# Straight-line batches and a re-ordered batch head in a two-layer graph kernel

## What is computed

```python
feats = einsum('bnf,hfu->bhnu', X, W)              # 8 heads of 64
dense = leaky_relu(e_self[..., :, None] + e_neigh[..., None, :], 0.2)
att = softmax(dense + -1e10 * (1 - A))             # e_* = feats . a_*
out = relu(einsum('bhij,bhju->bhiu', att, feats) + b)
x = layernorm(x + out)
agg = einsum('bij,bjf->bif', adj, x) / max(sum(adj), eps)
x = layernorm(x + relu(einsum('bnf,of->bno', concatenate([x, agg]), W)))
```

## Time and profile before

| | |
|---|---|
| median of 3 runs | 3521.29 us (3521.27 to 3525.59) |
| the profiled execution | 3527.3 us, its span 3525.3 us |
| PE busy | 3383.6 us, 96% of the span |
| DVE / ACT / POOL busy | 2466.5 / 1870.4 / 284.8 us |
| mean granted TensorE clock | 0.985 of full speed |

### The profile page before, as it was taken

The page is one execution under the profiler, slowest core; times in us unless marked ns, Lnnn a source line. Parts: engine busy times, 40 slices in busy tenths (PEclk is TensorE's granted clock), DMA queues, the critical chain, the costliest instruction groups (busy, mean ns, idle before and its releaser), DMA issues.

```text
span 3525.3 us, 135227 instructions
## 1 busy us (share of the span) xinstructions
PE 3383.6 (96%) x58432; PEld 2881.7 (82%) x58432; DVE 2466.5 (70%) x4364; ACT 1870.4 (53%) x2457; POOL 284.8 (8%) x252
## 2 busy tenths in 40 slices
PE   5999999999999999999999999999999999999998
PEld 4978879787796878969789697887978879788795
DVE  4857668576685766858578585784857758577685
ACT  3736546365464645646456373563746547355463
POOL 0020200202001020010201002010020200202001
PEclk9999999999999999999999999999999999999999
DMA  4113131131321213112031221312213121131210
GB/s 170 52 43 117 39 103 56 50 99 38 103 64 55 93 35 106 64 54 93 29 113 57 67 81 32 117 50 81 68 37 119 43 97 52 44 116 39 85 34 25
DMA packets 98401, 248.46 MB, mean 70 GB/s; under 512 B 14720, under 2 KB 14720, under 8 KB 97792
## 3 DMA queue, kind: packets, MB, share of 16 engines
q1 hardware_dynamic: 97792, 239.38, 20.5%
HBM read 205.26 MB, written 34.08 MB: 68 GB/s over the span
## 4 chain that ended last, share of the span: by engine, by line
PE 85%; DVE 8%; issue 5%; ACT 1%; DMA 0%; SPq 0%; DVEq 0%; ACTq 0%; POOL 0%; POOLq 0%
PE six L887 70%; PE pair L887 10%; DVE xs L766 2%; DVE stats L771 2%; PE six L1023 2%; DVE feat L658 1%; PE pair L916 1%; PE six L916 1%; PE pair L924 1%; PE six L924 1%; DVE rs L779 0%; ACT x_parts L502 0%; DVE trl L647 0%; DVE nb L781 0%; DVE x_parts L636 0%
## 5 line engine op out<-in xcount | busy, mean ns | idle before, releaser
L887 PE MATMUL six<-rest,mask 128*128 128x65 bf16 x16384 | 1549.8, 195 | 4.2 <-issue 4.0
L887 PE MATMUL six<-x_parts,mask 128*128 128x65 bf16 x16384 | 1549.4, 192 | 1.9 <-issue 1.3
L887 PE MATMUL six<-third,mask 128*128 128x65 bf16 x16384 | 1549.3, 192 | 0.2
L887 PEld LDWEIGHTS six<-x_parts,mask 128*128 128x128 fp8e4 x16384 | 1536.0, 97 | 8.9 <-issue 7.6
L887 PEld LDWEIGHTS six<-third,mask 128*128 128x128 fp8e4 x16384 | 1536.6, 98 | 0.0
L887 PEld LDWEIGHTS six<-rest,mask 128*128 128x128 fp8e4 x16384 | 1530.7, 96 | 6.9 <-issue 5.6
L479 ACT ACTIVATE step<-s_bc,n_step 128x1024 uint16<-128x1024 f32 x1024 | 1093.5, 1137 | 382.1 <-DVE mask L716 381.8
L716 DVE TENSOR_TENSOR mask<-adj_t,step 128x1024 uint16<-128x1024 uint16 x1024 | 651.3, 685 | 22.6 <-ACT step L479 22.6
L887 PE MATMUL six<-adj_t,x_parts 128*128 128x512 fp8e4 x1536 | 388.1, 380 | 7.1 <-ACT x_parts L502 5.6
L422 POOL TENSOR_TENSOR s_bc<-feat,rden 128x512 f32<-128x512 f32 x112 | 123.9, 1111 | 2998.0 <-DVE s_bc L759 2969.2
L887 PEld LDWEIGHTS six<-adj_t,x_parts 128*128 128x128 f16 x1536 | 146.4, 98 | 184.8 <-issue 23.6
(11 more groups left out here) (124 smaller groups left out, 4954.1 us busy)
## 6 DMA issues: line engine op xcount, KB each, us to landing
s_bc<-self_scores SPq DMA_DIRECT2D x128, 512.0 KB, 3.7
adj_nat<-in_adj_dram SPq DMA_DIRECT2D x96, 512.0 KB, 3.8
xs<-in_x_dram SPq DMA_DIRECT2D x128, 256.0 KB, 2.8
out_dram<-mask SPq DMA_DIRECT2D x128, 256.0 KB, 3.3
adj_nat<-in_x_dram SPq DMA_DIRECT2D x64, 256.0 KB, 5.0
step<-in_x_dram SPq DMA_DIRECT2D x64, 256.0 KB, 3.6
mask<-in_adj_dram SPq DMA_DIRECT2D x32, 512.0 KB, 5.0
xs<-in_L_gnn_W_dram SPq DMA_DIRECT2D x1, 2048.0 KB, 11.2
```

What stands on the lines that cost most here:

```text
L887: return pe.matmul(o, l, r, start=start, stop=stop, skip_group_check=True)
```

## The change

1. No engine loops over batches: each engine's code for the 16 batches is written out one after the other. With the loops the register arithmetic of the waits goes, and the `stand` increments are removed from all engines.
2. PE's batch begins with `features(b, 4)` (it waits for `o_sum` of tile 6 of the batch before, which frees bank 4), then `scores(b, 1)` in bank 5 in place of 6, then `features(b, 5)` in bank 6 in place of 5, in pieces: two chunks, the 8 transposes, one chunk, the small product (bank 3 in place of 6), the last chunk. The waits for `o_sum` and `o2_sb` of the last tile stand ahead of `features(b, 5)`, not at the end of the batch before.
3. `turn_x1(0)` comes after tile 2 of `aggregate_first`, not after tile 1.
4. DVE does `x_low(b + 1, 7)` before the sum of `ln1(7)`, not behind it.

```diff
-    FT_BANKS = (0, 1, 4, 5, 4, 5, 4, 5)
+    FT_BANKS = (0, 1, 4, 5, 4, 6, 4, 5)
+    SC_BANKS = (6, 5)
+    MAX_BANK = 3
...
-                dve.tensor_copy(nmax[:], bank[6][:, 0:SC]).then_inc(chain.sem, tick())
+                dve.tensor_copy(nmax[:], bank[MAX_BANK][:, 0:SC]).then_inc(chain.sem, tick())
...
+                    if more and t == T - 1:
+                        x_low(b + 1, T - 1)
                     dve.wait_ge(o2_sb.sem, o2_sb.at(b, t + 1))
                     dve.tensor_tensor(z[:, s], bank[O1_BANKS[s]][:], o2s[:, s], ALU.add).then_inc(o_sum.sem, 1)
-                    if more and t == T - 1:
-                        x_low(b + 1, T - 1)
...
             def batch(b, more):
 
+                if b >= 1:
+                    pe.wait_ge(o_sum.sem, o_sum.at(b - 1, T - 1))
+                features(b, 4)
+                pe.wait_ge(ft_sb.sem, ft_sb.at(b, HALF))
+                scores(b, 1)
+                if b >= 1:
+                    pe.wait_ge(o_sum.sem, o_sum.at(b - 1, T))
+                    pe.wait_ge(o2_sb.sem, o2_sb.at(b - 1, T))
                 pe.wait_ge(sc_f32.sem, sc_f32.at(b, 1))
-                scores(b, 1)
-                features(b, 4)
+                features(b, 5, range(0, 2))
                 pe.wait_ge(sc_f32.sem, sc_f32.at(b, 2))
-                stand(pe)
                 for t in range(T):
                     ins = pe.transpose(bank[2][:, t * SC:(t + 1) * SC], sc_row[:, col(t)], ident[0:SC, 0:SC])
                 ins.then_inc(nat_ps.sem, 1)
+                features(b, 5, range(2, 3))
                 pe.wait_ge(diag_ok.sem, diag_ok.at(b, 1))
-                mm(bank[6][:, 0:SC], ones16[:], diag16[:], True, True).then_inc(max_ps.sem, 1)
-                features(b, 5)
+                pe.wait_ge(at_sb.sem, at_sb.at(b, T - 1))
+                mm(bank[MAX_BANK][:, 0:SC], ones16[:], diag16[:], True, True).then_inc(max_ps.sem, 1)
+                features(b, 5, range(3, KC))
...
-                    if jt == 1:
+                    if jt == 2:
...
-                    pe.wait_ge(o2_sb.sem, o2_sb.at(b, T))
-                    pe.wait_ge(o_sum.sem, o_sum.at(b, T))
...
-            with pe.Fori(0, B - 1) as b:
-                batch(b, True)
-            batch(B - 1, False)
+            for b in range(B):
+                batch(b, b + 1 < B)
```

More of the change, by code:

```diff
@@ L358, in _ @@
                 load_late_adj(0, t)
-            with sp.Fori(0, B - 1) as b:
+            for b in range(B - 1):
                 first_scores(b)
@@ L466, in score_rows @@
                 half = slice(i * HALF * P, (i + 1) * HALF * P)
-                copy(sc_row[:, half], bank[6][0:SC, :]).then_inc(sc_f32.sem, 1)
+                copy(sc_row[:, half], bank[SC_BANKS[i]][0:SC, :]).then_inc(sc_f32.sem, 1)
             def batch(b, more):
@@ L574, in _ @@
                 degrees(0, t)
-            with act.Fori(0, B - 1) as b:
-                batch(b, True)
-            batch(B - 1, False)
+            for b in range(B):
+                batch(b, b + 1 < B)
         @block.vector
@@ L879, in _ @@
                 adj_rows(0, t)
-            with dve.Fori(0, B - 1) as b:
-                batch(b, True)
-            batch(B - 1, False)
+            for b in range(B):
+                batch(b, b + 1 < B)
         @block.tensor
@@ L926, in turn_adj, with features @@
                 ins.then_inc(at_ps.sem, 1)
[L928 to L931, removed]
-                c = t % HALF
-                split_product(bank[FT_BANKS[t]][:], [trh[:, k, col(c)] for k in range(KC)],
-                              [trl[:, k, col(c)] for k in range(KC)], [w0h[:, k, :] for k in range(KC)],
-                              [w0l[:, k, :] for k in range(KC)]).then_inc(ft_ps.sem, 1)
+            def features(b, t, chunks=range(KC)):
+                if 0 in chunks:
+                    pe.wait_ge(xt_lo.sem, xt_lo.at(b, t + 1))
+                    if t >= 4:
+                        pe.wait_ge(ft_sb.sem, ft_sb.at(b, t - 1))
+                c = t % HALF
+                ins = split_product(bank[FT_BANKS[t]][:], [trh[:, k, col(c)] for k in chunks],
+                                    [trl[:, k, col(c)] for k in chunks], [w0h[:, k, :] for k in chunks],
+                                    [w0l[:, k, :] for k in chunks], first=0 in chunks, last=KC - 1 in chunks)
+                if KC - 1 in chunks:
+                    ins.then_inc(ft_ps.sem, 1)
             def scores(b, i):
                 pe.wait_ge(xt_lo.sem, xt_lo.at(b, (i + 1) * HALF))
-                split_product(bank[6][:], [wah_wide[:, k * SC:k * SC + P] for k in range(KC)],
+                split_product(bank[SC_BANKS[i]][:], [wah_wide[:, k * SC:k * SC + P] for k in range(KC)],
                               [wal_wide[:, k * SC:k * SC + P] for k in range(KC)],
```

14 lines of the change are left out of this document (removed).

## The result

The kernel after takes **3409.6 us** (median of 4 runs, 3404.98 to 3412.62) against 3521.61 us before (4 runs, 3521.27 to 3525.59): the ratio is 0.9678, with an interval of 0.9662 to 0.9695. Forecast were 3406 us, in a range of 3392 to 3430. The profiled execution took 3408.76 us, of which 3406.6 us are its span; before, the span was 3525.3 us. So there are 118.7 us of span to account for.

What follows compares the result with a forecast made beforehand. PE, busy 96% of the span, was taken as the bound, with stops and slow clock at batch borders. Gains 102.2 + 3.4 + 12.5 - 3 = 115.1 us off 3527.3 give 3412, less 6.0 for the median: 3406 us, range 3392 to 3430.

Steps and rivals of the forecast that it cites:

- The term of the heads: Batch starts on PE: 102.2 us gained at 14 looped borders, 3.4 at the last, 0 at batch 0.
- The new head: PE from last adjacency transposes to first key product: no stop left, full clock, 15.2 us (bounds 14.9 to 15.74).
- the sign: Evidence that would show the forecast right: total PE busy lower by some 25 to 30 us as slow products go.
- The split of a border: Looped batch borders on PE: 3.85 us of each come from the jump, 3.45 from the order.
- The loops of the other engines at nothing: DVE, ACT and SP in their loops: slack exceeds the cost, so straight code there gains nothing.
- DVE, ACT and SP have slack: Key tiles: PE takes 1.5 us a tile, these engines have more slack than register work costs; gain nothing.
- The register arithmetic: Register work and `stand` in the key tiles: removal gains nothing, as batch 15 without registers keeps the same pace.
- `turn_x1(0)` one tile later: Second layer on PE: tile 2's aggregations cover a wait; 0.89 us in 14 batches, 12.5 us gained (bounds 0 to 13.4).
- The masks uncovered: First key tiles, tightest at tile 7: less cover for masks from scores through DRAM; 0.2 us a batch, 3 us lost.
- The rival that the masks become the bound: First key tiles: scores' DRAM trip makes all late by 1.3 us, not 0.2; 17 us, 3423 us; chance 0.13.
- The fetch: PE's instruction fetch: straight code fetched once per batch, as a looped batch is; nothing, 5 us either way.
- The slower rival: PE's instruction fetch: straight code starves PE; gain gone at 0.23 us a block, some 3850 us at 0.9; chance 0.03.

Runs made afterwards that it cites:

- after_again: The kernel after, unchanged, run once more beside other variants on the same chip; 3410.04 us, ratio 0.9642 to the kernel before.
- e6: The kernel after with the old order and banks of the batch head on PE, still straight code; 3422.61 us, ratio 0.968.
- e1: The kernel before with only the batch loops of all five engines written out and `stand` left out, old order kept; 3446.07 us, ratio 0.9747.
- before_again: The kernel before, unchanged, run once more on the third chip for another trace; 3530.41 us.
- e3: The kernel after with SP, POOL, ACT and DVE looping again, `stand` at their waits, PE straight; 3440.07 us, ratio 0.9731.
- e2: The kernel after with only PE looping over batches 1 to 14, `stand` back at its register waits; 3490.48 us, ratio 0.9868.
- e4: The kernel after with `turn_x1(0)` back behind tile 1 of `aggregate_first`; 3424.9 us, ratio 0.9681.
- e5: The kernel after with DVE's sum of tile 7 ahead of the low part again; 3416.42 us, ratio 0.9662.
- e7: The kernel after, with PE waiting for feature tile 1's bank only ahead of the sixth product of the first aggregation; 3403.01 us, ratio 0.962.

## Why the prediction was right, and which step of it wasn't

The predicted 3406 us was 3.6 us off the median of 3409.6, and the 115.1 us of the sum compare with 118.7 in the spans and 112.0 in the medians. That closeness is in part luck. The term of the heads (105.6 us) came out 2.2 too high, that of the turn 2.5 too low, and 3.3 us came from the key tiles behind tile 7, which had no term. And on the chip of `after_again` the same two kernels lie 128 us apart (3538.07 and 3410.04). Step by step:

- **The new head: right.** 15.2 us forecast, 15.37 measured. The cuts of features 5 cost 0.14 us, not 0.2: e6, with features 5 in one piece, is busy for 15.23 us in a head. The other pieces, 15.0 in the forecast, were 0.23 too low. The clock is 1.00 in every head, as forecast; PE's busy time fell by 38.3 us, of which 29.8 in the heads, where 25 to 30 was the sign. The looped borders gave 22.50 - 15.38 = 7.12 us each, 99.7 in all (forecast 102.2), and the last 3.28 (forecast 3.4).
- **The split of a border into 3.85 us for the jump and 3.45 for the order: wrong**, though its sum held. It took the last border's 18.65 us as the yardstick for "no jump", and one border is one draw: its scores ran at half the clock for 3.4 us, where the same stop without a jump left the clock alone in all 15 heads of e1 and in the last of `before_again`. The jumps are 5.5 us, the order 1.64 (0.63 from the low part ahead of the sum, 1.01 from features 4 ahead of the scores). The prediction's own figures at the first border pointed there: the stop of 5.3 us and the 1.7 us of slow scores make 7.0, the old order's own wait is 1.8 of them by e1, and that leaves 5.2 for the jump. The forecast of the whole didn't depend on the split, but that of each part did: the heads of e1 were expected 25 us too long.
- **The loops of the other engines at nothing: wrong**, hidden by the same sum. With the new order and PE in straight code DVE's jump comes to light: e3 costs 31 us. Before, PE's own stop covered it, for DVE's first work behind its jump then waited for the scores, which PE's stop had made late:

```profile
292.62 0.67 DVE L678 TENSOR_REDUCE nmax<-sc_row 16x1 f32<-16x512 f32 x1 [3.52 <-ACT sc_row L444]
```

  The step "DVE, ACT and SP have slack" read a mean over a batch, where the one place behind the jump mattered.
- **The register arithmetic: not told apart.** That straight code would do no harm was right; e1's key tiles from 7 on are 4.6 us shorter in sum than before. e2, with registers, the jump and `stand` on PE, is 13 us longer there, and which of these three makes its 75 short stops wasn't tried. PE's queue fetches 31 or 32 blocks in nearly all of its looped batches, where the kernel after has 28 or 29.
- **`turn_x1(0)` one tile later: right, somewhat low.** 12.5 us forecast, 15.0 in the stretch, 14.9 by e4. It gave 1.00 us a batch and not 0.89, in 15 batches and not 14.
- **The masks uncovered: right in kind, the size partly by chance.** 3 us of loss forecast, 3.2 measured in the stretch to key tile 7. But only some 1.5 us of it are masks: in 7 batches of the trace after, the first product of tile 7 comes 0.06 us behind the end of its mask. Three stops by "issue" ahead of that tile make 2.3 us more, which no term had. The kernel before has no late mask there. In the second looped head of the trace after, DVE no longer stands idle at `feature_rows(7)`, where it had 1.01 us before:

```profile
502.69 0.69 DVE L704 TENSOR_TENSOR mask<-adj_t,step 128x1024 uint16<-128x1024 uint16 x1 [1.21 <-ACT step L468]
...
504.50 0.68 DVE L646 TENSOR_TENSOR feat<-six,bias_bc 128x512 f32<-128x512 f32 x1
```

  The rival that the masks become the bound didn't come about; e5 shows how near it was, since the sum of 0.68 us ahead of the low part costs 5 us there.
- **The fetch: within its bounds.** The slower rival, straight code that starves PE, fell: all "issue" waits of the trace after come to 10.9 us, 0.024 us for each of the 458 blocks, where it decided from 0.23. That a looped batch is fetched too, and not held, is borne out: without any loop the count is lower (458 against 499), not higher.

## What to carry to other kernels

A loop around a long body can have a price on each engine that loops; here it was 2.5 to 4.1 us on PE and 2.5 to 3.2 on DVE. Read it at the first instruction behind the jump as an idle time by "issue", and see who waits for that engine there, before you take one engine's jump away alone. When the same place comes many times and one of them without the thing you want to price, look at its granted clock before you take it as the yardstick. And a short "issue" in front of a product that needs a bank may be the wait for the engine that empties it. In the trace after the two kinds could be told by the instruction queue: the stops of the fetch ended 2.2 to 2.5 us behind the begin of a block, those for the bank 7.8 us and more. Putting another place of the group first gave 7 us.

## What the runs showed of the hardware that I had not expected

- **The clock doesn't fall behind every stop of the same length.** In e1, 15 stops of 1.8 us left it at 1.00; the same stop at the last border of the kernel before brought 3.41 us at 1.2 GHz. In e3, stops of 1.2 to 1.9 us brought it down at 9 of 14 borders, and the length didn't decide: it fell behind one of 1.26 us and held behind one of 1.52; in e6, stops of 1.1 us never did. The jumps of e2, at 2.5 us and up, did at 12 of 13. What decides between them no run here shows, and I leave it open.
- **Straight code also has stops of the fetch.** The trace after has 25 short ones in the key tiles, 9.3 us in all, and the kernel before 53, 13.2 us. Of those of straight code about half (11 of 23 of over 0.06 us) sit at the very same product in `after_again`. They go with PE's instruction queue: the trace after has 13 stops by "issue" of over 0.15 us in the key tiles, and each of them ends 2.2 to 2.5 us behind the begin of a block, of which there is one in some 7 us. The 14 such stops at the first aggregation end 7.8 to 16.2 us behind the last block; those are the waits for a bank that e7 took away.
- **A chip can be slower for one kernel and not for another.** The kernel before took 3521, 3529, 3537 and 3538 us in four groups, that after 3409.6 and 3410.0. The second trace of the kernel before has more short stops in the key tiles (84, 17.2 us) and one more head at a clock of 0.85; that the straight kernel has less that can vary so fits this, and is argued only.
